# A four-layer sequence model: the state-space layers' products with B, C, the convolution and the D term put on other engines

## The reference

```python
h = _layernorm(x, gamma, beta) * (1.0 + scale) + shift
xm, z = jnp.split(h @ W_in, 2, axis=-1)              # 512 channels each
xm = silu(conv(xm, conv_w, taps=4) + conv_b)         # per channel, causal
dtr, Bm, Cm = jnp.split(xm @ W_xp, [64, 80], axis=-1)  # 64, 16, 16
dt = jax.nn.softplus(dtr @ W_dt + b_dt)
def step(hst, inp):                                  # over 512 tokens
    dt_t, B_t, C_t, x_t = inp
    dA = jnp.exp(dt_t[:, :, None] * A)
    hst = hst * dA + (dt_t * x_t)[:, :, None] * B_t[:, None, :]
    return (hst, jnp.einsum('bds,bs->bd', hst, C_t))
y = ys + xm * D_param
return x + gate * ((y * silu(z)) @ W_out)
```

## Time and profile before

| | |
|---|---|
| runs, us | 3856.5 median of 3 (3854.93 to 3887.91) |
| profiled execution, us | 3873.2 span; mean granted TensorE clock 0.830 |
| busy, share of the span | PE 75%, DVE 72%, ACT 54%, POOL 44% |
| first scan of a batch, layer 1 | 514.7, 648.3, 788.2, 929.4, 1068.9, 1208.7, 1348.7, 1488.6; last scan ends 1588.5 |
| first scan of a batch, layer 3 | 2665.9, 2802.1, 2956.2, 3109.8, 3263.4, 3417.0, 3570.6, 3724.2; last scan ends 3823.5 |

### The profile page before, as it was taken

How to read it: one execution, slowest core, us unless ns; L and a number is a source line. 1 busy time by engine, 2 the same in 40 slices (tenths; PEclk the granted TensorE clock), 3 DMA queues, 4 the chain that set the end, 5 groups by cost and what they waited for, 6 DMA issues and landing times. The chain is left out here.

```text
span 3873.2 us, 38272 instructions
## 1 busy us (share of the span) xinstructions
PE 2902.1 (75%) x11060; PEld 1488.6 (38%) x11060; DVE 2801.5 (72%) x3410; ACT 2089.7 (54%) x3166; POOL 1716.0 (44%) x1209
## 2 busy tenths in 40 slices
PE   6999667877777877468788878866776866867775
PEld 4555333444444444222333322223434434434443
DVE  1333279999999999755555555515999989999996
ACT  0223267777777777213444444426766756767663
POOL 0000047678677768800000000003767667677686
PEclk7899787988988988768888888768887978878888
DMA  2000111111011101043333333010101011111011
GB/s 78 11 33 22 47 39 44 39 44 50 28 44 50 50 23 55 33 82 63 60 39 66 66 61 61 12 58 33 43 24 60 30 53 50 39 45 61 23 55 49
DMA packets 101857, 176.64 MB, mean 46 GB/s; under 512 B 10219, under 2 KB 88827, under 8 KB 92563
## 3 DMA queue, kind: packets, MB, share of 16 engines
q1 hardware_dynamic: 97430, 161.65, 15.8%
q0 software_dynamic: 4224, 12.59, 1.0%
HBM read 139.69 MB, written 34.12 MB: 45 GB/s over the span
## 5 line engine op out<-in xcount | busy, mean ns | idle before, releaser
L965 POOL TENSOR_TENSOR l_h<-l_h,l_c_all 128x512 f32<-128x512 f32 x1024 | 1483.1, 1465 | 709.6 <-DVE l_h L896 688.5
L896 DVE TENSOR_TENSOR_SCAN l_h<-l_dA,l_ps_dbu 128x512 f32<-128x512 f32 x1024 | 1210.1, 1205 | 137.2 <-PE l_ps_dbu L1089 81.8
L1089 PE MATMUL l_ps_dbu<-ident,l_dub 128*128 128x128 f32 x4096 | 691.8, 303 | 282.8 <-DVE l_h L896 256.9
L767 ACT ACTIVATE l_dub<-l_duT,l_b_tok 128x512 f32<-128x512 f32 x1024 | 723.6, 711 | 281.5 <-PE l_ps_dbu L1089 281.5
L1089 PEld LDWEIGHTS l_ps_dbu<-ident,l_dub 128*128 128x128 f32 x4096 | 520.2, 154 | 783.0 <-DVE l_h L896 535.5
L781 ACT ACTIVATE l_dA<-l_dt,l_a_neg 128x512 f32<-128x512 f32 x1024 | 724.1, 711 | 0.2
L1076 PE MATMUL l_ps_y<-l_h,ident 128*128 128x512 f32 x1024 | 630.2, 702 | 104.5 <-DVE l_h L864 103.9
L1346 DVE TENSOR_REDUCE l_q_max<-l_ring 128x2 f32<-128x1024 f32 x256 | 312.7, 1224 | 335.7 <-PE l_ring L1614 332.9
L1499 ACT ACTIVATE l_probs<-l_ring 128x1024 f32<-128x1024 f32 x256 | 261.7, 1024 | 433.3 <-PE l_ring L1623 432.3
L864 DVE TENSOR_TENSOR l_h<-l_h 128x512 f32<-128x512 f32 x512 | 459.8, 901 | 26.1 <-POOL l_h L965 26.0
L925 POOL DMA_INDIRECT l_x_in<-x_dram,l_idx_x x32 | 33.2, 1038 | 951.8 <-DMA l_idx<-in_idx 938.7
(11 more groups left out here) (181 smaller groups left out, 3049.2 us busy)
## 6 DMA issues: line engine op xcount, KB each, us to landing
l_c_all<-c_rows_dram SPq DMA_DIRECT2D x64, 1024.0 KB, 4.8
l_res<-x_dram SPq DMA_DIRECT2D x24, 512.0 KB, 5.4
parts_dram<-l_parts SPq DMA_DIRECT2D x48, 256.0 KB, 2.8
l_qs<-parts_dram SPq DMA_DIRECT2D x48, 256.0 KB
l_ks<-parts_dram SPq DMA_DIRECT2D x48, 256.0 KB
l_x_in<-x_dram SPq DMA_DIRECT2D x16, 512.0 KB, 5.3
x_dram<-l_res SPq DMA_DIRECT2D x16, 512.0 KB, 3.0
su_cond_w<-in_cond_w SPq DMA_DIRECT2D x1, 5120.0 KB, 15.1
```

The source lines that it names most:

```text
L767: return act.activation(dub[:, n % 2, t, :], duT[:, p, t, :], ACT.Copy, scale=b_tok[:, p, t, n:n + 1])
L896: dve.tensor_tensor_scan(h[:, h_slot(s), :], dA[:, s % DA_RING, :], ps_dbu[:, dbu_slot(s), :], 0.0, ALU.mult, ALU.add).then_inc(scan_ok, 1)
L965: pool.tensor_tensor(h[:, h_slot(s), :], h[:, h_slot(s), :], c_all[:, (n // C_GROUP) % 2, n % C_GROUP, :], ALU.mult).then_inc(hc_ok, 1)
L1089: last = pe.transpose(ps_dbu[:, dbu_slot(s), t * P:(t + 1) * P], dub[:, n % 2, t, j * P:(j + 1) * P], ident[:])
```

## The change

B goes into a matrix: ACT makes diag(B) of 128 tokens (ident scaled per partition, 128x128, a ring of 4) and PE multiplies duT with it, four products in place of four transposes. POOL multiplies two units by the row of C in one instruction of 128x1024. The states' sum goes to PE entirely: one identity matmul per unit, 64 per batch, SUM_LAG 10; `add_states` is gone. The convolution is four matmuls per block with diagonal matrices of its taps (conv_diag), its bias added by ACT as it reads PSUM; the D term is a matmul with d_diag into ps_y. Both are built by POOL at the layer's start. silu_gate moves from POOL to DVE and reads ps_y. clip, softplus, dt_max and dt_u work on all four blocks at once. The gate's row is loaded per batch, not for all batches at the start. The steps' places change: ln_stats goes to s = 0, ln_apply to 4.

```diff
-DA_RING, DBU_RING = 8, 3
-PAIRED = UNITS // 2
-ADD_LAG, SUM_LAG = 3, 7
+DA_RING, DBU_RING, H_RING, DIAG_RING = 8, 3, 16, 4
+SUM_LAG = 10
 ...
-                        sp.wait_ge(hc_ok, b * UNITS + (g - 1) * C_GROUP * JB + CREDIT)
+                        sp.wait_ge(hc_ok, b * H_PAIRS + (g - 1) * GROUP_PAIRS)
 ...
+                    sp.dma_start(gate[:], io["gates"][gate_at, bass.ds(b, 1), :].to_broadcast([P, D])).then_inc(gate_ld, 16)
 ...
+                def conv_part(b, j):
+                    act.wait_ge(cv_mm, b * JB + j + 1)
+                    if j == 0 and not first(b):
+                        act.wait_ge(dt_ok, b)
+                    act.activation(work[:, j, :], misc[:], ACT.Identity, bias=vec(vecs, L + "_conv_b")[:, j:j + 1]).then_inc(cv_ok, 1)
 ...
+                def softplus(b):
+                    act.wait_ge(clip_ok, b + 1)
+                    act.activation(work[:], work[:], ACT.Exp).then_inc(dt_exp, 1)
+                    act.wait_ge(dt_exp, b + 1)
+                    act.activation(work[:], work[:], ACT.Ln, bias=1.0).then_inc(ln_ok, 1)
 ...
+                    if s == 3: ln_rstd(b)
+                    if s in (7, 9): mod(b, (s - 7) // 2)
+                    if s in (11, 13, 15, 17): x_part(b, (s - 11) // 2)
+                    if s in (19, 21, 23, 25): conv_part(b, (s - 19) // 2)
+                    if s in (27, 29, 31, 33): z_part(b, p, (s - 27) // 2)
+                    if s == 34: silus(b, p)
+                    if s == 39: xd(b, p)
+                    if s == 41: b_copy(b, p)
+                    if s in (43, 45, 47, 49): dt_raw(b, (s - 43) // 2)
+                    if s == 54: softplus(b)
+                    if s in (60, 61, 62, 63): du_tok(b, p, s - 60)
 ...
-                    return act.activation(dub[:, n % 2, t, :], duT[:, p, t, :], ACT.Copy, scale=b_tok[:, p, t, n:n + 1])
+                    last = act.activation(diag[:, n % DIAG_RING, t, :], ident[:], ACT.Copy, scale=b_tok[:, p, t, n:n + 1])
 ...
+                def silu_gate(b, p, j):
+                    dve.wait_ge(sum_ok, b * UNITS + UNITS - JB + j + 1 + CREDIT)
 ...
+                    dve.tensor_tensor(y[:, j, :], ps_y[:, j, :], z[:, p, j, :], ALU.mult).then_inc(yg_ok, 1)
 ...
-                    if s == 7: ln_stats(b)
-                    if s == 10: ln_apply(b)
-                    if s in (18, 20, 22, 24): conv(b, (s - 18) // 2)
+                    if s == 0: ln_stats(b)
+                    if s == 4: ln_apply(b)
+                    if s == 50: clip(b)
+                    if s == 55: dt_max(b, p)
+                    if s == 56: dt_u(b, p)
 ...
-                    if s < ADD_LAG: add_states(b, UNITS - ADD_LAG + s)
-                    if s in (4, 5, 6, 7): y_skip(b, p, s - 4)
-                    if s in (48, 50): out_gate(b, (s - 48) // 2)
+                    if s in (5, 6, 7, 8): silu_gate(b, p, s - 5)
+                    if s == 35: out_gate(b, 0)
+                    if s == 51: out_gate(b, 1)
 ...
+                for k in range(JB * TAPS):
+                    c = VEC_LAYOUT[L + "_conv_w"][0] + k
+                    pool.tensor_scalar(conv_diag[:, k, :], ident[:], vecs[:, c:c + 1], None, ALU.mult)
+                for j in range(JB):
+                    last = pool.tensor_scalar(d_diag[:, j, :], ident[:], vec(vecs, L + "_D")[:, j:j + 1], None, ALU.mult)
 ...
+                        two = h[:, s % H_RING - 1:s % H_RING + 1, :]
+                        c_row = c_all[:, (n // C_GROUP) % 2, n % C_GROUP:n % C_GROUP + 1, :]
+                        pool.tensor_tensor(two, two, c_row.to_broadcast([P, 2, T]), ALU.mult).then_inc(hc_ok, 1)
 ...
+                    for k in range(TAPS):
+                        last = pe.matmul(misc[:], conv_diag[:, j * TAPS + k, :], conv_in[:, j, k:k + T], start=(k == 0), stop=(k == TAPS - 1))
 ...
+                    if s in (6, 8): xn_half(b, (s - 6) // 2)
+                    if s in (10, 12, 14, 16): x_side(b, (s - 10) // 2)
+                    if s in (18, 20, 22, 24): conv(b, (s - 18) // 2)
+                    if s in (26, 28, 30, 32): z_side(b, (s - 26) // 2)
+                    if s == 38: x_proj(b, p, after_post)
+                    if s == 40: b_turn(b, p)
+                    if s in (42, 44, 46, 48): dt_proj(b, p, (s - 42) // 2)
+                    if s in (59, 60, 61, 62): du_turn(b, s - 59, after_post)
 ...
+                    if n == 0:
+                        if not first(b):
+                            pe.wait_ge(yg_ok, b * JB - JB + j + 1)
+                        pe.matmul(ps_y[:, j, :], d_diag[:, j, :], u[:, j, :], start=True, stop=False, skip_group_check=True)
+                    if j % 2 == 0:
+                        pe.wait_ge(hc_ok, b * H_PAIRS + s // 2 + 1)
+                    pe.matmul(ps_y[:, j, :], ident[:], h[:, s % H_RING, :], start=False, stop=(n == N - 1), skip_group_check=True).then_inc(sum_ok, 1)
 ...
-                            last = pe.transpose(ps_dbu[:, dbu_slot(s), t * P:(t + 1) * P], dub[:, n % 2, t, j * P:(j + 1) * P], ident[:])
+                            last = pe.matmul(ps_dbu[:, dbu_slot(s), t * P:(t + 1) * P], duT[:, p, t, j * P:(j + 1) * P], diag[:, n % DIAG_RING, t, :],
+                                             start=True, stop=True)
 ...
-                        if has_post and s in (47, 49):
-                            out_proj(b - 1, (s - 47) // 2)
+                        if has_post and s == 34:
+                            out_proj(b - 1, 0, has_prep)
+                        if has_post and s == 50:
+                            out_proj(b - 1, 1, has_prep)
```

More of the change, by code:

```diff
@@ L609, in early, with last_of @@
             return isinstance(b, int) and b < 2
+        def last_of(b, k):
+            return isinstance(b, int) and b == B - k
         def batches(eng, body):
@@ L793, in _ @@
                     prep_step(s, 0, 0)
+                for t in range(TB):
+                    diagonal(0, 0, 0, t)
                 batches(act, body)
@@ L820, in ln_apply @@
                     last.then_inc(xn_ok, 1)
-                def conv(b, j):
-                    dve.wait_ge(xc_ok, b * JB + j + 1)
-                    if j == 0 and not first(b):
-                        dve.wait_ge(dt_ok, b * JB)
-                    wcol = VEC_LAYOUT[L + "_conv_w"][0] + j * TAPS
-                    dve.tensor_scalar(work[:, j, :], conv_in[:, j, 0:T], vecs[:, wcol:wcol + 1],
-                                      vec(vecs, L + "_conv_b")[:, j:j + 1], ALU.mult, ALU.add).then_inc(prep_v, 1)
-                    for k in range(1, TAPS):
-                        dve.wait_ge(prep_v, b * PREP_V + 1 + j * (TAPS - 1) + k)
-                        last = dve.scalar_tensor_tensor(work[:, j, :], conv_in[:, j, k:k + T], vecs[:, wcol + k:wcol + k + 1], work[:, j, :],
-                                                        ALU.mult, ALU.add)
-                        last.then_inc(prep_v if k < TAPS - 1 else conv_ok, 1)
@@ L845, in dt_max, with clip @@
[L845 to L855 removed]
+                def clip(b):
+                    dve.wait_ge(dti_ok, b * JB + JB)
+                    dve.wait_ge(u_ok, b * 2 + 1)
+                    dve.tensor_scalar(work[:], dt_in[:], 30.0, None, ALU.min).then_inc(clip_ok, 1)
@@ L969, in _ @@
                 batches(pool, body)
-                for j in range(JB):
-                    silu_gate(B - 1, (B - 1) % 2, j)
                 if gathered:
```

256 lines of the change are left out of this document (109 added, 147 removed).

## The result

The changed kernel takes 4307.8 us (median of 4 runs, 4290.7 to 4310.4) beside 3861.6 us of the kernel before on the same chip: ratio 1.1135, 95% interval 1.109 to 1.118. The forecast was 4290 (4170 to 4400), slower. Its profiled execution has a span of 4288.9 us, 415.7 over the 3873.2 of before; the medians lie 446.2 apart. The profile of after is the fastest of its runs and that of before 16.7 us above its median, so the 30 us between 415.7 and 446.2 belong to the executions that were profiled and not to the change.

A forecast was written before the change was run, and what follows sets the result against it. The prediction took DVE to set the pace before and PE after, at 160.2 us per middle batch plus stalls. Layer 1's +246 and layer 3's +192 made +438 on 3856.5 us, so 4290 us (range 4170 to 4400).

The forecast's parts named there:

- The term 160.2: PE's work per middle batch, never waiting and at full clock: 160.2 us, above the batches' 139.8 and 153.6.
- (a): ln_stats at s=0 waits for the load of x: PE stalls 5.0 us in layer 1, 10.6 in layer 3.
- (b): ln_apply at s=4 ends after PE wants it for xn_half at s=6: 2.4 us per middle batch.
- (c): dt_max and dt_u at s=55, 56, each behind a POOL pair: PE waits 1.7 us at du_turn, s=59.
- (d): Weight loads on PE not hidden at a wait: 0.5 us per middle batch.
- (e): TensorE clock's return after an idle time, once per batch: 1.7 us.
- First batch: Layers 1 and 3, no output projection, ten sums fewer: 150 us, +16.5 and +13.5.
- Preparation: Ahead of each layer's first batch, convolution on PE and softplus in one piece: +20 us; layer 3 with diagonals +26.
- R1: Rival: PE's clock does not rise from 0.88 and 0.82, giving 4540 us; with R4 beyond 4400, chance 0.13.
- R2: Rival: the stalls vanish and PE's bare work stays, +231, 4088 us; chance 0.11.
- R3: Rival: diagonal products stream like transposes, 0.44 us for four, giving 3760 us; chance 0.02 faster.
- R4: Rival: POOL's pairs starve DVE, +6 to 10 us a batch, 4400 us; with R1 beyond 4400, chance 0.13.

The follow-up runs named there:

- e1: Changed kernel with the convolution back on DVE and B multiplied in by ACT scaling ahead of PE transposes again: 3848.5 us, 0.9951 of the kernel before.
- e6: Changed kernel with x loaded early (for batch b + 2 in mid-batch b) and PE's eight batches written out instead of looped: 4199.0 us, ratio 1.0849.
- e5: Changed kernel with B by transposes, the convolution back on DVE and x loaded early: 3758.9 us, 0.9721 of the kernel before.
- e7: Changed kernel with B by transposes, convolution on DVE, x loaded early, and PE's batches written out instead of looped: 3759.4 us, ratio 0.9739.
- e3: Kernel before with only diag(B) and true products in place of scaling and transposes: 3917.2 us, ratio 1.0109.
- e2: Changed kernel with x for batch b + 2 loaded in the middle of batch b: 4200.5 us, ratio 1.0851.
- e8: Changed kernel with B by transposes, early x, convolution on DVE one operation per scan, z half at states 18 to 24: 3688.7 us, ratio 0.9540.

## Why the prediction was right

**PE as the bound.** Right, and by its price. The last batches, in which PE never waits, take 121.9 us; less D term and output projection (3.4 + 6.9) that is 111.6 for 64 sums and the 63 groups of products that lie between first and last scan: 0.86 and 0.90 us, 1.76 per state, forecast 1.75. The price of an f32 product was taken from eight of them in layer 0, 0.224 each; e1 measured the difference to a transpose as 28.6 us per batch, by the forecast's prices 28.7. The term 160.2 is borne out by e6, whose middle batches with no wait for x and no loop take 163.1 to 164.1, 1.2 of it at du_turn; the other 2 to 3 us were not taken apart. The forecast's "256 diagonals" on ACT are 64 per batch (row of L775: 1024 in all, 0.388 us each); its 26 us are those of 64, and nothing hung on it, since ACT was busy 83 us of 170.

**The stalls, term by term.** (a) The wait for x: forecast 5.0 and 10.6 with 0.8 at dbu(0) in each, measured 5.4 and 10.3 in the two batches shown, by the very path told ahead: c load, x load behind it, landing at +7.5 for +7.2. But it stood in four of six middle batches of layer 1, not in all. (b) xn_half, forecast 2.4: it isn't there in those batches. While PE stands for x, ln_apply follows the statistics and is in time; the term was double counting with (a). It shows where (a) is absent (1.5 in one batch, 2.8 in the first ones). (c) du_turn: 1.2 measured, 1.7 forecast. (d) The 0.5 for weight loads at a wait has no row behind it, and no run shows it by itself. (e) The clock's return: the forecast took 1.7 per batch; the clock was at its lower level for 1 to 11 us of a middle batch in layer 1 (5.7 in the mean) and for 7 to 14 in layer 3 (10.8), and half of that is lost. Together (c) to (e) came out larger than forecast, (b) smaller, and the two stops at the loop, 4.6 and 3.3 us together, which the sum did not have, took the place of the wait for x in the batch behind. The sum of a middle batch is within 1.3 us in both layers, in part because misses offset each other.

**Ends.** First batch: forecast 150, measured 158.4. The step that failed is that it would only lose work: without an output projection of the batch before, ScalarE's two SiLUs stand uncovered and PE stops for 3.4 us at the products behind them; 2.8 at xn_half and 0.9 at dbu(2) are the rest with the clock's return. Last batch: 121.9 for 124; the sum's 1.4 over its named terms was not there. The first batch's +8.4, the last's -2.1 and six times -0.9 nearly cancel, so layer 1's batches came to +229.6 for +230.7. The tail:

```profile
1828.79 8.75 PE L1067 MATMUL l_ps_y<-l_h,ident 128*128 128x512 f32 x20
1829.04 1.22 DVE L868 TENSOR_TENSOR_SCAN l_h<-l_dA,l_ps_dbu 128x512 f32<-128x512 f32 x1 [0.53 <-PE l_ps_dbu L1082]
...
1838.32 3.72 PE L1044 MATMUL l_misc<-l_w_out,l_y 128*128 128x256 f32 x16 [0.78 <-DVE l_y L840]
```

From the scans' end (1830.26) to the output projection 8.1 us pass; forecast 5.4. The forecast had "a pair, two sums and a gate", but SUM_LAG is 10, and PE still has ten whole sums (twenty instructions) to do. Before it was 10.7.

**Preparation.** Against the two profiles the sum of 438 is 22 us too large (against the medians' 446 it is 8 too small), and nearly all of the 22 lies in the stretches ahead of the layers' first scans, +12.2 and +8.5 for +20 and +21. But the preparation itself was not cheaper. First statistics and first scan, layer 1 and the statistics of layer 3, in the changed kernel, then layer 1 in the kernel before:

```profile
432.11 1.41 DVE L808 BATCH_NORM_STATS2 l_stats<-l_x_in 128x6 f32<-128x256 f32 x4 [2.42 <-DMA l_x_in<-x_dram]
526.86 1.22 DVE L868 TENSOR_TENSOR_SCAN l_h<-l_dA,l_ps_dbu 128x512 f32<-128x512 f32 x1 [10.92 <-PE l_ps_dbu L1082]
...
2822.65 1.40 DVE L808 BATCH_NORM_STATS2 l_stats<-l_x_in 128x6 f32<-128x256 f32 x4 [16.60 <-DMA l_x_in<-x_dram,l_idx_x]
```
```profile
446.21 1.41 DVE L808 BATCH_NORM_STATS2 l_stats<-l_x_in 128x6 f32<-128x256 f32 x4 [2.10 <-DMA l_x_in<-x_dram]
514.74 2.33 DVE L896 TENSOR_TENSOR_SCAN l_h<-l_dA,l_ps_dbu 128x512 f32<-128x512 f32 x2 [11.37 <-PE l_ps_dbu L1089]
```

68.5 us became 94.8, +26.2 for a forecast of 20; in layer 3 it is 2822.65 to 2916.2, 93.5 for 69.0, +24.5. The convolution's four steps on PE took 17.9 (forecast 17.6); under-priced was the dt chain (dt_proj to du_turn 18.7 for 14.3, +4.4, forecast 2.4), and 4.9 us had no term: the input projection's four steps ahead of the convolution took 16.0 for 12.1, three of them with the clock at its lower level where it had been one, and x_proj to dt_proj 8.0 for 6.9. What hides it is the time ahead of the statistics, 14.1 us shorter in layer 1, and in layer 3 16.0 shorter from layer 1's last scan on, though the diagonals lie in it. The layers there are untouched, and e5 and e7, equal but for PE's loop, have their first statistics at 454.2 and 425.9. So the miss of 22 us is no finding on the change: terms too small by 6 us in layer 1 and by 10 in layer 3, diagonals with them, were covered by a spread between executions of 15 and more, and the forecast's sum had no place for that.

The diagonals on POOL took 607 ns each, not 0.3; a small operation on POOL does not shrink with its columns as the 1.25 us of 128x512 was made to:

```profile
L884 POOL TENSOR_SCALAR l_conv_diag<-ident,vecs 128x128 f32<-128x128 f32 x32 | 18.9, 607 | 926.0 <-POOLq L94 926.0
```

With d_diag's, twenty such operations stand ahead of layer 3's first gather, 11.7 us for the forecast's 6.

**The clock and the rule.** In the changed kernel the granted clock is 0.96 to 1.00 in the batches, near the full clock that the sum took, and R1 (4540) is refuted. Before the prediction no row parted the transposes from the waits as the cause of the 0.88 and 0.82. Now e1's last batch does: four transposes per state, a third of PE's time, next to f32 sums and without a stop, at a granted clock of 1.00. e3 has 0.96 and 0.92 with products in the rhythm of before, but there PE also has 28.7 us more work in a batch. The Trainium skill (TensorE: Matmul & The Clock Gate, Part 4) says that the transpose mode does not count as PE being busy in the same way as a product; by the row of e1, transposes mixed with sums without a stop did not keep the clock down, and what they would do alone no run here shows.

**The rivals.** R2 (4088): e2 and e6 took the stalls away and reached 4200. Its mechanism is real for (a), but it counted the first batches without their own waits (158.4 for 146), 160.2 without the 3 us that remain, and 20 us for the preparations of both layers, which took 26 and 25 more. R3 fell with e3 and e1: four products cost 0.89, above its deciding 0.58. R4 (4400) did not come: clip, dt_max and dt_u took 1.79, 2.32 and 3.18 us beside POOL's pairs, where four of an add's mean would be 3.6, and DVE has some 75 us to spare in each batch. Its mechanism was not wrong, only covered: in e8, with less work on PE, PE waits 2.4 us longer at the layer norm in three of six middle batches of layer 3.

## What to carry to other kernels

Price work that is moved to a matrix engine by its own form and type (an f32 product against a transpose of the same size is 0.224 to 0.109 us here), add it up for one stage, and compare with the pace of the engine that sets it now: two moves that fit by themselves (the products in e3, with PE at about 117 us per batch, and the full sums with the D term in e8, at about 118) did not fit together with the convolution, at 160. Where two engines lie as close together as the 118 and 106 us of e1 and e5, totals did not give the time (144 and 136 passed); look for rows of work on the follower that are longer than the ring between them covers, and for loads queued behind the last work of a stage. The relief of DVE was worth having (0.954 of the kernel before in e8) when only the sums, the D term and the gate moved (with POOL's pairs), x was loaded early and the convolution was spread.
